# Gated graph network on one core: shared-edge counts as a fifth product of each counting round

## The reference

```python
h = jnp.maximum(_layernorm(x), 0.0) @ lin_w.T + lin_b
for i in range(3):
    m = h @ weight[i]
    agg = jax.ops.segment_sum(m[src], dst, num_segments=12500)
    h = gru_cell(agg, h, w_ih, w_hh, b_ih, b_hh)
return x + h
```

## Time and profile before

| what | value |
|---|---|
| median of three runs | 3803.09 us |
| the profiled execution | 3803.88 us, span 3802.1 us |
| instructions | 76,920 |
| busy: TensorE, ScalarE, VectorE, GpSimd | 88%, 80%, 74%, 70% |
| counting stage | about 210 to 1310 us of the span |
| rounds counted | 1470 + 210 of four products, 210 of two |

### The profile page before, as it was taken

How to read it: one execution, slowest core, us unless ns; L and a number is a source line. 1 busy time by engine, 2 the same in 40 slices (tenths; PEclk the granted TensorE clock), 3 DMA queues, 4 the chain that set the end, 5 groups by cost and what they waited for, 6 DMA issues and landing times.

```text
span 3802.1 us, 76920 instructions
## 1 busy us (share of the span) xinstructions
PE 3361.6 (88%) x24880; PEld 2652.7 (70%) x24881; DVE 2801.6 (74%) x7778; ACT 3044.4 (80%) x4427; POOL 2663.4 (70%) x2622
## 2 busy tenths in 40 slices
PE   5279888998999799999799999999987999999997
PEld 4156666666666577777577777777776877787775
DVE  7678787888887677777577777777775777777775
ACT  4268898888888788888788889888886888878784
POOL 4677776776766677775177777777736777777775
PEclk8589999999999899999899999999998999999999
DMA  8345545455554697776666777777775766666674
GB/s 273 112 120 191 175 156 181 148 184 166 164 184 145 194 275 213 212 212 187 196 199 201 219 207 217 218 207 214 210 226 180 207 203 202 205 201 205 200 210 126
DMA packets 445139, 736.12 MB, mean 194 GB/s; under 512 B 63688, under 2 KB 329032, under 8 KB 444744
## 3 DMA queue, kind: packets, MB, share of 16 engines
q1 hardware_dynamic: 206616, 402.21, 32.7%
q0 software_dynamic: 122880, 251.82, 24.5%
q10 hardware_dynamic: 115248, 77.10, 6.5%
HBM read 557.22 MB, written 173.67 MB: 192 GB/s over the span
## 4 chain that ended last, share of the span: by engine, by line
POOL 35%; PE 23%; issue 15%; ACT 15%; DVE 6%; DMA 4%; ACTq 1%; DVEq 0%; SPq 0%; POOLq 0%
POOL ring_region L600 34%; PE psum L903 16%; ACT wide_counts L717 10%; ACT half_counts L758 3%; DMA states<-temps 2%; DVE quad_onehots L1370 2%; PE psum L920 2%; PE psum L880 1%; PE psum L868 1%; DVE block_onehots L1354 1%; PE psum L811 1%; DVE temps L1330 1%; DMA messages_region<-counts 1%; PE psum L804 0%; ACTq L745 0%
## 5 line engine op out<-in xcount | busy, mean ns | idle before, releaser
L600 POOL DMA_INDIRECT ring_region<-messages,edge_src x2560 | 2609.2, 1019 | 1037.5 <-issue 764.2
L717 ACT CAST wide_counts<-messages_region 128x1024 fp32r<-128x1024 uint8 (+1 forms) x1596 | 1762.0, 1185 | 188.5 <-PE psum L920 155.1
L920 PE MATMUL psum<-wide_counts,message_halves 128*128 128x512 f32 x7448 | 1794.4, 398 | 70.3 <-DVE message_halves L1406 50.5
L920 PEld LDWEIGHTS psum<-wide_counts,message_halves 128*128 128x128 f32 x7448 | 1397.6, 191 | 374.8 <-ACT wide_counts L717 90.0
L903 PE MATMUL psum<-quad_onehots,block_onehots 128*128 128x266 bf16 (+1 forms) x6720 | 844.7, 272 | 104.2 <-ACT half_counts L758 63.8
L758 ACT CAST half_counts<-psum 128x490 f32 (+1 forms) x1680 | 846.9, 594 | 64.6 <-PE psum L903 40.2
L903 PEld LDWEIGHTS psum<-quad_onehots,block_onehots 128*128 128x128 bf16 x6720 | 576.4, 100 | 359.5 <-issue 137.0
L1406 DVE TENSOR_TENSOR message_halves<-messages_region,message_halves 128x256 fp32r<-128x256 f32 (+1 forms) x1596 | 751.0, 471 | 55.0
L1404 DVE CAST message_halves<-messages_region 128x256 fp32r<-128x256 f32 (+1 forms) x1596 | 611.4, 383 | 114.1 <-PE psum L920 75.7
L1370 DVE TENSOR_SCALAR quad_onehots<-iota_quad,count_keys 128x1176 bf16<-128x1176 f16 x960 | 560.7, 645 | 0.0
L880 PE MATMUL psum<-onehot,ring_region 128*128 128x36 bf16 x7680 | 245.0, 179 | 151.7 <-DMA ring_region<-messages,edge_src 140.8
(11 more groups left out here) (132 smaller groups left out, 1788.4 us busy)
## 6 DMA issues: line engine op xcount, KB each, us to landing
messages_region<-counts SPq DMA_DIRECT2D x532, 462.0 KB
counts<-half_counts SPq DMA_DIRECT2D x210, 462.0 KB
ring_region<-messages,edge_src POOLq DMA_INDIRECT x2560
messages<-pieces_out ACTq DMA_DIRECT2D x98, 192.0 KB
messages_region<-plain SPq DMA_DIRECT2D x21, 896.0 KB, 8.0
temps<-states ACTq DMA_DIRECT2D x98, 128.0 KB
states<-temps ACTq DMA_DIRECT2D x98, 128.0 KB
plain<-temps ACTq DMA_DIRECT2D x98, 128.0 KB
```

Source lines behind the costliest of these rows:

```text
L600: nc.gpsimd.indirect_dma_start(out=rows[:, n % RING, h * QC + c, :], out_offset=None, in_=messages[layer], in_offset=bass.IndirectOffsetOn ...
L717: nc.scalar.copy(wide_counts[:, v % UBUF, here], stage[v % ABUF][:, here, :, 0:WW]).then_inc(s_wide, 1)
L920: mm = nc.tensor.matmul(psum[:, 6 + kg % 2, 0:2 * WW], halves[:, v % UBUF, b % HB, half * P:(half + 1) * P], wide_counts[:, v % UBUF, b % ...
```

## The change

The eighth round goes. All rounds are alike: four products as before, and in the 210 quads with a quad in front a fifth one, of 14 columns, which adds the shared edges of this round's 14 blocks to the first column of each block's window. The copy takes all 36 columns (504 elements) in every round. There are 1680 rounds in the same 90 steps. SyncE now waits before each of the seven stores of a half for the copy of that round only.

```diff
-    COUNTED = [(j, i) for j in range(BUILDS) for i in range(ROUNDS + (j % HQ > 0))]
-    COUNTED_AT = ...
-    COUNTED_BY = ...
+    BUILD_ROUNDS = BUILDS * ROUNDS
...
-        return min(max(s - BUILD_FROM, 0) * len(COUNTED) // (last - BUILD_FROM), len(COUNTED))
+        return min(max(s - BUILD_FROM, 0) * BUILD_ROUNDS // (last - BUILD_FROM), BUILD_ROUNDS)
...
-        return 0 if done == 0 else min(COUNTED[done - 1][0] + 2, BUILDS)
+        return 0 if done == 0 else min((done - 1) // ROUNDS + 2, BUILDS)
...
-                sp.wait_ge(s_ev, COUNTED_BY[HQ * g + HQ - 1])
                 for i in range(ROUNDS):
+                    sp.wait_ge(s_ev, ROUNDS * (HQ * g + HQ - 1) + i + 1)
                     sp.dma_start(counts[k, 2 * i:2 * i + 2, :, half]...
...
             def evacuate(e):
-                j, i = COUNTED[e]
+                j, i = e // ROUNDS, e % ROUNDS
...
                 act.wait_ge(s_bld, e + 1)
-                counted = psum[:, COUNT_BANKS[e % 3], :]
                 if j % HQ:
-                    act.wait_ge(s_ev, COUNTED_AT[j - 1, min(i, ROUNDS - 1)] + 1)
-                if i < ROUNDS:
-                    own = 1 if j % HQ else 0
-                    nc.scalar.copy(half_counts[half][:, 2 * HB * i:2 * HB * (i + 1), own:WS][
-                                       :, :, bass.ds(columns[j], W - own)],
-                                   counted[:, 0:RW].rearrange("p (b w) -> p b w", w=W)[:, :, own:W]).then_inc(s_ev, 1)
-                else:
-                    nc.scalar.copy(half_counts[half][:, :, bass.ds(columns[j], 1)],
-                                   counted[:, 0:NB].unsqueeze(2)).then_inc(s_ev, 1)
+                    act.wait_ge(s_ev, e + 1 - ROUNDS)
+                nc.scalar.copy(half_counts[half][:, 2 * HB * i:2 * HB * (i + 1), bass.ds(columns[j], W)],
+                               psum[:, COUNT_BANKS[e % 3], 0:RW].rearrange("p (b w) -> p b w", w=W)).then_inc(s_ev, 1)
...
             def count_round(e):
...
-                if i == ROUNDS:
-                    pe.wait_ge(s_xshare, j - j // HQ)
-                    first_column = xs[j % 2][0].rearrange("p (b w) -> p b w", w=SUBW[0])[:, :, 0]
-                    nc.tensor.matmul(counted[:, 0:NB], blocks_oh[j % 3][:, 0, :], first_column, start=True, stop=False)
-                    nc.tensor.matmul(counted[:, 0:NB], blocks_oh[(j - 1) % 3][:, QC - 1, :], shared_oh[j % 2],
-                                     start=False, stop=True).then_inc(s_bld, 1)
-                    return
                 by_block = ...
                 for k, c in enumerate(SUBORDER):
                     ...
+                if j % HQ:
+                    pe.wait_ge(s_xshare, j - j // HQ)
+                    mm = nc.tensor.matmul(by_block[:, :, 0], blocks_oh[(j - 1) % 3][:, QC - 1, :],
+                                          shared_oh[j % 2][:, 2 * HB * i:2 * HB * (i + 1)], start=False, stop=True,
+                                          skip_group_check=True)
                 mm.then_inc(s_bld, 1)
...
-                    pe.wait_ge(s_ev, len(COUNTED))
+                    pe.wait_ge(s_ev, BUILD_ROUNDS)
...
-                    dve.wait_ge(s_bld, COUNTED_BY[j - 2])
+                    dve.wait_ge(s_bld, ROUNDS * (j - 1))
```

More of the change, by code:

```diff
@@ L94, in gated_graph_layers @@
     BUILDS = NSB * DQ
-    COUNTED = [(j, i) for j in range(BUILDS) for i in range(ROUNDS + (j % HQ > 0))]
-    COUNTED_AT = {round_of: e for e, round_of in enumerate(COUNTED)}
-    COUNTED_BY = [max(e for e, (quad, _) in enumerate(COUNTED) if quad == j) + 1 for j in range(BUILDS)]
+    BUILD_ROUNDS = BUILDS * ROUNDS
     PARTS = NB // (2 * HB)
@@ L890, in count_round @@
                     pe.wait_ge(s_ev, e + 1 - len(COUNT_BANKS))
-                counted = psum[:, COUNT_BANKS[e % 3], :]
-                if i == ROUNDS:
-                    pe.wait_ge(s_xshare, j - j // HQ)
-                    first_column = xs[j % 2][0].rearrange("p (b w) -> p b w", w=SUBW[0])[:, :, 0]
-                    nc.tensor.matmul(counted[:, 0:NB], blocks_oh[j % 3][:, 0, :], first_column, start=True, stop=False)
-                    nc.tensor.matmul(counted[:, 0:NB], blocks_oh[(j - 1) % 3][:, QC - 1, :], shared_oh[j % 2],
-                                     start=False, stop=True).then_inc(s_bld, 1)
-                    return
-                by_block = counted[:, 0:RW].rearrange("p (b w) -> p b w", w=W)
+                by_block = psum[:, COUNT_BANKS[e % 3], 0:RW].rearrange("p (b w) -> p b w", w=W)
                 for k, c in enumerate(SUBORDER):
```

## The result

The changed kernel takes 3748.2 us (median of four runs, 3743.9 to 3754.0) against 3802.6 for the kernel before, timed in turn with it: a ratio of 0.9855, 95% interval 0.9833 to 0.9877. Timed again on another chip it was 0.9859 (0.9838 to 0.9879). So it is 54 us faster; 77 were forecast (3726 us).

What follows compares the result with a forecast made beforehand. Counting rounds, paced by the ring of three banks, were taken to bound the counting stage. Rounds 88, VectorE -10, GpSimd -1, stores +2 make 79 us saved: 3724.9, said as 3726 us; own range 3708 to 3748, wider 3706 to 3780.

Steps and rivals of the forecast that it cites:

- A: Rival at TensorE: the fifth product's weight load is not hidden; 0.51 us a round, gain 44 us, 3758 us; chance 0.10.
- C: Rival at VectorE: one-hot builds take the eighth round's place; half of 88 us becomes waits, 3758 us; chance 0.08.
- The eighth round: Counting stage: removing it frees a turn of the ring of banks in 210 quads, 0.4725 us each, 99 us.
- The fifth product and the longer copy: Counting rounds: each adds 0.01 us to the ring; a quad takes 3.36 instead of 3.78 us, 88 us saved.
- The ring: Three banks between TensorE's products and ScalarE's copies: 1.44 us long after the change, a third of it, 0.480, per round.
- VectorE's charge of 10 us: Heads of steps: builds have 0.13 us left per quad, not 0.55, so TensorE waits more for one-hots: 10 us lost.
- The stores: SyncE's stores start earlier, nothing waits behind them; the last half's hand-over to the first dense product gets 2 us shorter.
- GpSimd, later stages: Gathers stay out of the chain, jitter costs 1 us, stage 1022 us; later stages move up with their length unchanged.
- The floor of 1003 us: Counting stage: gathers at 1.070 us plus 0.29 us issue leave GpSimd 97 us to spare, so 1100 can't fall below 1003.
- D: Rival at GpSimd: gathers slowed to 1.12 us bound the stage at 1042 us, 3744 us; milder forms within the forecast's 0.70.
- B: Rival at TensorE: the fifth product costs 0.16 us and makes TensorE the bound, 44 us slower, 3846 us; chance 0.06.
- its sign, over 80 us at the weight loads: Profile sign of the one-hots rival: TensorE's weight loads wait over 80 us for quad one-hots instead of 36.

Runs made afterwards that it cites:

- the runs on the fifth product: Changed kernel without the fifth product: 3746.8 us (ratio 0.9859 to the kernel before); with it issued twice: 3753.4 us (0.9866).
- the move: VectorE makes the tanh's input behind the step's first build, not behind all: changed kernel 3723.7 us (0.9787), kernel before 3791.1 us (0.9961).
- with VectorE's work lightened as well: Changed kernel, tanh input made behind the step's first build, shared one-hots left out for all quads but the first two: 3716.6 us (0.9782).
- with the input moved, in either place: Changed kernel with VectorE making the tanh's input behind the step's first build, 3723.7 us (0.9787), or ahead of its last, 3728.9 us (0.9808).

## Why the prediction was right, and where it was not

**The number.** 3748.2 us lies at the edge of the range that went with the forecast itself (3708 to 3748). The wider range, 3706 to 3780, holds it well, but that room was left for the rivals A and C, which did not happen. To that extent the number was lucky.

**The eighth round.** Right in the main: its place in the row of rounds was what it cost, and it came back. But all 210 were priced at 0.4725 us. Behind 59 of them the next round was not held by a copy, and there an eighth round takes 0.23 us of TensorE (589.82 to 590.05 in the earlier trace rows). As an estimate, 14 of the 99 us were never there.

**The fifth product and the longer copy.** Right in kind and nearly in size: an unbroken quad is 0.393 us shorter, not 0.42, so 0.393 x 210 = 83 us are saved where I had 88. The ring (0.144 + 0.594 + 0.111 + 0.608) was forecast at 1.44 us and is 1.457, but its length is not what sets the spacing with three banks, as the runs on the fifth product show. That it came out so near is in part luck.

**VectorE's charge of 10 us.** This step failed. I looked for the loss at TensorE's waits for builds, and they became shorter (36.3 to 20.7 us at the weight loads). The loss went through the third engine: an input that VectorE makes behind a build, a tanh that waits for it, and the copies queued behind the tanh. The prediction priced the builds by their length against a quad's; it did not ask what else stands behind the last build of a step and which queue waits for that. The change made this wait about 13 us more expensive, by the runs with the input moved.

**The stores.** They gave their 2 us at the hand-over. That nothing waits behind them was wrong: ScalarE's 30 register loads grew from 31 to 53 us beside them, which cost the stage about as much, by the one run with the old wait.

**GpSimd, later stages.** The gathers stayed out of the chain, with 70 us in hand, not 20, since the stage came to 1050 us and not 1022. The floor of 1003 us was no floor: it took a gather at 1.070 us, and in the runs after the change it is 1.007 to 1.056 (1.035 in the changed kernel, so that D, with slower gathers, is excluded, although its 3744 us came near). The stages behind the turn moved up as a block, within the 13 us by which their length varies from profile to profile.

**The sum.** The counting stage, first copy to last, became 50.5 us shorter (1099.0 to 1048.5), where 77 were forecast. From the two profiles, 83 us were gained by the rounds and 12 by shorter waits for builds (rounds that start at a build's end, over the regular spacing: 25 us before, 13 after). So some 45 were lost: 13 behind the tanh, as tested, with the uncertainty said there; about 14 that the eighth rounds never cost and about 4 for the clock (below), both estimates; 2 to 3 beside the stores. These can overlap, and about 10 us stay open. The rivals A and B are excluded by the runs without and with two fifth products. C, the one-hots, named a loss of that size but not its place: its sign, over 80 us at the weight loads, did not come (20.7).

**Better than both.** The changed kernel with the move, 3723.7 us, is 2.1% under the kernel before. GpSimd waits for its ring for 40 us there, but that is no fixed limit to what faster counting could give: with VectorE's work lightened as well the stage was 5 us shorter and GpSimd waited 62.

## What to carry to other kernels

If producers and consumers share a ring of buffers, an item costs the ring's length over the number of buffers, or the time that the slower side needs for it, and neither need be shorter for a small item (here a copy of 98 elements lasts as long as one of 490): merge small items into the others, even at the price of more instructions. Compare the same item before and after, for items of one kind can differ by more than the change. Then look at what stands behind the last long job of each step, on every engine: its time to be ready does not shrink with the step, and the queue that waits for it may be a third engine's. When a transfer is started earlier, see what it then runs beside. A wait ended by VectorE does not mean that VectorE has too much to do; see first what VectorE itself was waiting for.

## What the runs showed of the hardware

After TensorE's stall of 2.55 us ahead of 621.09 its granted clock fell to half, 1.2 GHz, for 3.4 us. The stretches before, in and behind it in the changed kernel (columns as in the earlier trace rows):

```profile
616.00:621.00 5.00, 2.55 (x46) 2.20 (x44) 4.80 (x15) 2.66 (x7) 3.78 (x5) 1.00 0.24 68
621.00:625.00 4.00, 3.91 (x27) 3.11 (x28) 2.94 (x10) 3.23 (x6) 3.09 (x4) 0.57 0.30 84
625.00:629.00 4.00, 4.00 (x44) 3.32 (x41) 3.70 (x10) 3.86 (x8) 2.36 (x3) 1.00 0.29 83
```

and the rounds in it start 0.82 us apart:

```profile
621.69 0.95 PE L886 MATMUL psum<-quad_onehots,block_onehots 128*128 128x266 bf16 x4
...
622.51 0.95 PE L886 MATMUL psum<-quad_onehots,block_onehots 128*128 128x266 bf16 x4
```

In 3.4 us that is 4.1 rounds instead of 6.9, 1.4 us lost. The counting stage has 8 such spells in the kernel before, 11 in the one after, and 4 with the input moved, in either place. So a stall of TensorE can cost more than its own length; three more spells are about 4 us, as an estimate. Not every such stall is followed by a spell: in the changed kernel's counting stage TensorE stood still 32 times for 1.5 to 2.6 us, and all 11 spells begin at the end of one of these. That the stall brings the clock down was seen in the trace, not tested by itself.

The copy of 98 single bytes, one in each block's row, took 610 ns, as long as one of 490 elements in rows of 35: as bad a use of ScalarE as of the ring.

A load of eight register values on ScalarE took 0.54 to 0.57 us alone and up to 2.5 us beside the stores of counts. In the ten runs with the early stores and three banks or two the 30 loads take 51 to 58 us, in the three with the late stores 30 to 34. What the two share was not tested.
